# A scaled residual formed by two wide VectorE operations in place of four narrow ones

## The chip, the core and the metric

The kernel runs on one core of a Trainium2 chip. The metric is the device time of one execution in microseconds; the time given for a kernel is the median of its runs. Engines are named as the profile names them: PE is TensorE, DVE is VectorE, ACT is ScalarE, POOL is GpSimd.

## What is computed

A hybrid layer on 4 x 32 images of 128 x 128: Fourier layers with an attention over tokens, then a two-layer mixer, then attention and experts over rows. The part that the change touches is the first mixer layer:

```
def fno_layer(x, spec_w, skip_w, skip_b, out_shape, norm=None, act=None):
    xs = fourier_resample(conv1x1(x, skip_w, skip_b), out_shape)
    xf = spectral_conv(x, spec_w, out_shape)
    if norm is not None:
        xf = instance_norm(xf, *norm)
    y = xf + xs
    return act(y) if act is not None else y
...
m = fno_layer(m, mixer_w1, mixer_skip_w1, mixer_skip_b1, (H, W), norm=(mixer_norm_g1, mixer_norm_b1), act=_gelu)
```

With one channel, `conv1x1` is a scale and a shift of each image. The norms ahead of it are folded into the same two numbers, so `xs` is image times factor plus shift, with a factor and a shift per image. The inverse transform `xf` is added, and gelu follows.

## The kernel before

The kernel is a chain of stages, each a block with one program per engine; a stage starts when all engines have left the one before. The stage here is `stage_inverse` of kind 'mix1', between `stage_factors` and `stage_mixer`. The 128 images lie in SBUF as `m.b`, with 128 partitions (rows) and 128 columns an image. They are treated in 33 sets of images three apart: set b of quad q and remainder j holds images 12q+j, 12q+j+3 and so on; 30 sets hold four images, two hold three, one holds two. Three sets share one quad of the half-way result (eleven quads).

The order on each engine is written out by hand; semaphores tie the engines together. For a set b:

- DVE `linear(b)` (L1297) writes factor times image plus shift to `m.tmp`, which has two buffers, so it waits for the gelu of set b-2. The factor and the shift are columns 4 and 5 of `m.aff`, one number per image and the same on each partition.
- PE inverts the set into a bank of PSUM (L1177 to L1179, `second`); DVE `combine(b)` (L1331) adds gain times that to `m.tmp`.
- ACT takes gelu into `m.ust` (L1264), forms another scaled version of the images in place (`affine`, L1238), and copies out a forward transform (L1229).
- DVE takes statistics of the gelu (L1313); PE transforms it forward (L1187).
- POOL adds x from `m.a` to the images behind `affine` (L1143), then copies the gelu to `m.a` (L1146), which frees the buffer of `m.ust` for set b+2.
- Once in three sets the next quad's half-way result is split in two fp16 parts: ACT L1221, which stands behind the third set's gelu, affine and copy, then DVE L1282, which PE's next inversions need.

DVE's order is: linear(0), and then for each b linear(b+1), combine(b), statistics(b-1), and behind each third set L1282.

The names in the rows: `modes` is `m.tmp`, `images_b` is `m.b`, `transposed` holds `m.aff` and the statistics, `ow_stats_and_image_stage` is `m.ust`, `half_inverse_low` and `half_inverse_high` are the two halves.

Of the kernel before, what the change touches and what calls it, by code (L numbers as in the profile page):

```python
# [27 lines left out]
ALU = mybir.AluOpType  # L28
# [4 lines left out]
NB, NT, NH, NW = 4, 32, 128, 128  # L33
# [124 lines left out]
def over(ap, axis, n):  # L158

    shape = list(ap.shape)  # L160
    return ap.unsqueeze(axis).to_broadcast(shape[:axis] + [n] + shape[axis:])


def semaphores(nc, held, stage, names):

    made = {n: nc.alloc_semaphore(f"{stage}_{n}") for n in names.split()}
    held.extend(made.values())
    return Names(made)
# [872 lines left out]
def stage_inverse(nc, held, m, kind, mix=None, ins=None):  # L1041


    s = semaphores(nc, held, "inverse_" + kind, "in0 in1 in2 in3 v sized rooted total scaled turned high low first bhigh "
                   "blow rows used lin ready saved forward copied weights cleared algebra affine added gstat partly")
# [5 lines left out]
    def images(store, b):  # L1051
        q, j, gs = sets[b]
        return store[:, 12 * q + j:12 * q + j + 3 * len(gs) - 2:3, :]

    def width(b):
        return len(sets[b][2])

    def spread(flat, n):
        return flat[:, 0:n * NW].rearrange("p (t w) -> p t w", t=n)

    def turned(r):
        n = len(COEF_BANKS[r])
        return m.ps[2 + r % 6][0:FM, 0:n * P].rearrange("p (t x) -> p t x", x=n)
# [47 lines left out]
    with nc.Block() as block:  # L1111
        @block.sync
        def _(sp):
            if kind == 'proj':
                mix_img = mix.rearrange("t h w -> h t w")
                for q in range(QUADS):
                    if q >= 4:
                        sp.wait_ge(s.used, 3 * (q - 3))
                    t = slice(12 * q, min(NI, 12 * q + 12))
                    sp.dma_start(m.b[:, t, :], mix_img[:, t, :]).then_inc(arrived[q % 4], 16)  # L1120
                    if q == 3:
                        sp.wait_ge(s.cleared, 1)
                        load_mixer(sp, m, ins, 1, s.weights)
            if kind == 'mix1':
                x_img = ins['x'].rearrange("b t h w -> h (b t) w")
                for q in range(QUADS):
                    t = slice(12 * q, min(NI, 12 * q + 12))
                    if q >= 4:
                        sp.wait_ge(arrived[q % 4], 16 * (q // 4))
                    sp.dma_start(m.a[:, t, :], x_img[:, t, :]).then_inc(arrived[q % 4], 16)  # L1130
                load_mixer(sp, m, ins, 2, s.weights)
                sp.wait_ge(s.weights, 32)
# [142 lines left out]
        @block.vector  # L1275
        def _(vec):
            c = Chain(vec, s.v)

            def half(q):
                vec.wait_ge(s.bhigh, q + 1)  # L1280
                whole = min(4, (NI - 12 * q) // 3) * NW
                e = vec.tensor_tensor(m.halfL[:, q % 2, 0:whole], m.ps[q % 2][0:3 * FM, 0:whole], m.halfH[:, q % 2, 0:whole],  # L1282
                                      ALU.subtract)
                if q == QUADS - 1:
                    tail = slice(whole, whole + NW)
                    e = vec.tensor_tensor(m.halfL[0:2 * FM, q % 2, tail], m.ps[q % 2][0:2 * FM, tail],
                                          m.halfH[0:2 * FM, q % 2, tail], ALU.subtract)
                e.then_inc(s.blow, 1)

            def linear(b):  # L1290

                if b >= 2:
                    vec.wait_ge(s.ready, b - 1)
                q, j, gs = sets[b]
                for i in range(len(gs)):
                    img = 12 * q + j + 3 * i
                    e = vec.tensor_scalar(m.tmp[:, b % 2, i * NW:i * NW + NW], m.b[:, img, :], m.aff[:, 4, img:img + 1],  # L1297
                                          m.aff[:, 5, img:img + 1], ALU.mult, ALU.add)
                e.then_inc(s.lin, 1)

            def statistics(b):
                vec.wait_ge(s.used, b + 1)
                q, j, gs = sets[b]
                for i in range(len(gs)):
                    img = 12 * q + j + 3 * i
                    vec.bn_stats((m.st if kind == 'mix2' else m.stat)[:, img, :], m.b[:, img, :])

            def gelu_statistics(b):
                vec.wait_ge(s.ready, b + 1)
                q, j, gs = sets[b]  # L1310
                for i in range(len(gs)):
                    img = 12 * q + j + 3 * i
                    e = vec.bn_stats(m.stat[:, img, :], m.ust[:, b % 2, i, :])  # L1313
                e.then_inc(s.gstat, 1)

            def combine(b):
                vec.wait_ge(s.rows, b + 1)
                n = width(b)
                y = spread(m.ps[2 + b % 4], n)
                if kind == 'proj':  # L1320
                    if sets[b][1] == 0:
                        q = sets[b][0]
                        vec.wait_ge(arrived[q % 4], 16 * (q // 4 + 1))
                    x = images(m.b, b)
                elif kind == 'mix1':
                    vec.wait_ge(s.lin, b + 1)
                    x = spread(m.tmp[:, b % 2], n)
                else:
                    vec.wait_ge(s.partly, b + 1)
                    x = images(m.b, b)  # L1330
                vec.scalar_tensor_tensor(out=x, in0=y, scalar=gain, in1=x, op0=ALU.mult, op1=ALU.add).then_inc(s.used, 1)  # L1331

            if kind == 'proj':
                g = m.coef.rearrange("p x y -> p (x y)")
                vec.tensor_tensor_reduce(m.square, g, g, 1.0, 0.0, ALU.mult, ALU.add, m.col[:, 24:25]).then_inc(s.sized, 1)
                vec.wait_ge(s.total, 1)
                vec.tensor_scalar(m.col[:, 27:28], m.ps[0][:, 0:1], 2.0 ** -18, 1e-30, ALU.mult, ALU.add).then_inc(s.scaled, 1)
                vec.wait_ge(s.rooted, 1)
                vec.reciprocal(up, down).then_inc(s.scaled, 1)
                vec.wait_ge(s.scaled, 2)  # L1340
            for r, xs in enumerate(COEF_BANKS):
                vec.wait_ge(s.high, r + 1)
                n = len(xs)
                dst, high = (t[:, :, xs[0]:xs[0] + n] for t in (m.coefL, m.coefH))
                vec.scalar_tensor_tensor(out=dst, in0=turned(r), scalar=up[0:FM] if kind == 'proj' else 1.0, in1=high,
                                         op0=ALU.mult, op1=ALU.subtract).then_inc(s.low, 1)
            half(0)
            half(1)
            if kind == 'mix1':
                linear(0)  # L1350
            for b in range(len(sets)):
                if kind == 'mix1' and b + 1 < len(sets):
                    linear(b + 1)
                combine(b)
                if b >= 1:
                    (gelu_statistics if kind == 'mix1' else statistics)(b - 1)
                q, j, _ = sets[b]
                if j == 2 and q + 2 < QUADS:
                    half(q + 2)
            (gelu_statistics if kind == 'mix1' else statistics)(len(sets) - 1)  # L1360
# [1268 lines left out]
```

## Time and profile before

| what | value |
|---|---|
| median of three runs | 2350.61 us (2346.66 to 2353.24) |
| the profiled execution | 2354.32 us, span 2352.4 us |
| DVE busy in the span | 1882.0 us, 80% |
| PE busy | 2082.6 us, 89% |
| ACT busy | 1665.1 us, 71% |
| POOL busy | 602.9 us, 26% |

The stage of the change lasts from about 320 to 450 us of the span. The shares of the whole span say little on it, since most of the time belongs to the attention and the experts behind it; its own views are in the rows below. In a timeline, equal instructions of an engine that follow without a gap are merged: "x4" are four of them, and the time beside it runs from the start of the first to the end of the last. Two neighbours of an engine can overlap a little.

### The profile page before, as it was taken

The numbers are of one execution on the slowest core, as the hardware profiler recorded it, in microseconds if no ns is written. First come the engines' busy times: TensorE is split into PE (matmuls) and PEld (weight loads), VectorE is DVE, ScalarE is ACT, GpSimd is POOL, SyncE is SP. The second block draws the span as 40 slices with busy tenths as digits, with TensorE's granted clock in tenths as the row PEclk, the third lists the DMA queues.
The fourth block names the chain that finished last, engine by engine and source line by source line (L and its number), as shares of the span: only waits on it lengthen the run. The fifth ranks groups of instructions, "written<-read, shape, count | busy, mean of one in ns | idle before, by whom it ended". The sixth has DMA issues, their size and how long they took to land. (4 is left out here: it accounts for less than half of the span.)

```text
span 2352.4 us, 30833 instructions
## 1 busy us (share of the span) xinstructions
PE 2082.6 (89%) x10374; PEld 1067.8 (45%) x10374; DVE 1882.0 (80%) x3586; ACT 1665.1 (71%) x2413; POOL 602.9 (26%) x750
## 2 busy tenths in 40 slices
PE   7767859865899999999999999999999999767778
PEld 7722437732444444444444444444444444333333
DVE  4666887688778889889888888889888888867776
ACT  1444236464778888888888888878888888667666
POOL 1035415335302202102102102112000001046668
PEclk9978655555999999999999999999999999889999
DMA  9003560000000000000000000000000000000101
GB/s 301 9 1 143 153 151 3 1 1 6 1 10 1 1 1 1 1 1 1 1 1 1 1 1 1 1 1 1 1 1 1 1 1 1 0 14 28 32 28 46
DMA packets 80833, 55.72 MB, mean 24 GB/s; under 512 B 11283, under 2 KB 78739, under 8 KB 79140
## 3 DMA queue, kind: packets, MB, share of 16 engines
q1 hardware_dynamic: 75476, 52.38, 7.4%
q10 hardware_dynamic: 5200, 1.38, 0.3%
q8 instruction: 82, 1.34, 0.2%
q14 instruction: 75, 0.61, 0.1%
HBM read 36.91 MB, written 16.78 MB: 23 GB/s over the span
## 5 line engine op out<-in xcount | busy, mean ns | idle before, releaser
L2004 ACT ACTIVATE inner<-banks,key_bias,scales 128x1024 f32<-128x1024 f32 x512 | 617.2, 1205 | 212.5 <-PE banks L1821 207.3
L2189 DVE TENSOR_TENSOR weights_low<-weights,weights_high 128x1024 f16<-128x1024 f32 x512 | 674.4, 1317 | 17.0
L2011 ACT ACTIVATE weights<-inner 128x1024 f32<-128x1024 f32 x512 | 541.1, 1057 | 17.3 <-DVE weights_low L2189 1.6
L2185 DVE CAST weights_high<-weights 128x1024 f16<-128x1024 f32 x512 | 371.3, 725 | 175.8 <-ACT weights L2011 161.6
L2295 POOL CAST sums_high<-sums 128x512 f16<-128x512 f32 x32 | 39.1, 1221 | 1089.2 <-ACT sums L1983 1071.3
L1821 PE MATMUL banks<-queries_high,keys_high 128*128 128x512 f16 x1024 | 304.5, 379 | 0.7 <-ACT inner L2004 0.7
L1836 PE MATMUL banks<-weights_high,tokens_low 128*128 128x512 f16 x1024 | 304.6, 379 | 0.0
L1821 PE MATMUL banks<-queries_low,keys_high 128*128 128x512 f16 x1024 | 304.6, 379 | 0.0
L1821 PE MATMUL banks<-queries_high,keys_low 128*128 128x512 f16 x1024 | 304.6, 379 | 0.0
L1836 PE MATMUL banks<-weights_low,tokens_high 128*128 128x512 f16 x1024 | 304.6, 379 | 0.0
L1836 PE MATMUL banks<-weights_high,tokens_high 128*128 128x512 f16 x1024 | 304.5, 379 | 0.0
L2494 ACT ACTIVATE scaled<-banks,gates 128x128 f32<-128x128 f32 x512 | 149.2, 395 | 88.6 <-PE banks L2456 88.5
L1836 PEld LDWEIGHTS banks<-weights_high,tokens_low 128*128 128x128 f16 x1024 | 100.2, 98 | 120.9
L1821 PEld LDWEIGHTS banks<-queries_low,keys_high 128*128 128x128 f16 x1024 | 100.2, 98 | 120.9
L1836 PEld LDWEIGHTS banks<-weights_low,tokens_high 128*128 128x128 f16 x1024 | 100.2, 98 | 120.8
L1821 PEld LDWEIGHTS banks<-queries_high,keys_low 128*128 128x128 f16 x1024 | 100.2, 98 | 120.8
L1836 PEld LDWEIGHTS banks<-weights_high,tokens_high 128*128 128x128 f16 x1024 | 100.2, 98 | 120.8
L2454 PE MATMUL banks<-expert_weights_high,normed_high 128*128 128x512 f16 x256 | 103.3, 403 | 57.0 <-DVE residual_and_scaled L2530 43.7
L1821 PEld LDWEIGHTS banks<-queries_high,keys_high 128*128 128x128 f16 x1024 | 96.8, 98 | 91.3 <-ACT inner L2004 1.7
L2559 POOL TENSOR_TENSOR scaled_halves<-scaled 128x256 f32<-128x256 f32 x128 | 94.9, 741 | 93.4 <-ACT scaled L2494 93.0
L2530 DVE SCALAR_TENSOR_TENSOR residual_and_scaled<-banks,gates,residual_and_scaled 128x128 f32<-128x128 f32 x384 | 109.9, 341 | 0.1
L2455 PE MATMUL banks<-expert_weights_low,normed_high 128*128 128x512 f16 x256 | 103.2, 403 | 0.0
(613 smaller groups left out, 3243.0 us busy)
## 6 DMA issues: line engine op xcount, KB each, us to landing
images_b<-in_x SPq DMA_DIRECT2D x32, 256.0 KB, 9.4
images_a<-in_x SPq DMA_DIRECT2D x8, 1024.0 KB, 9.8
mixed_scratch<-images_a SPq DMA_DIRECT2D x4, 2048.0 KB, 13.1
result<-group_result SPq DMA_DIRECT2D x32, 256.0 KB, 2.3
images_b<-mixed_scratch SPq DMA_DIRECT2D x10, 768.0 KB, 5.2
images_a<-in_x SPq DMA_DIRECT2D x10, 768.0 KB, 9.1
mixer_weights<-in_L_conv_mixer_w SPq DMA_DIRECT2D x4, 272.0 KB, 6.8
table<-tables ACTq DMA_DIRECT2D x1, 772.5 KB, 7.1
```

Of the source, the lines that this page charges most:

```text
L1821: mm = pe.matmul(m.ps[2 * (t % 2) + h], key[:, par, part], query[:, q, 512 * h:512 * h + 512], start=(i == 0), stop=(i == 2))
L1836: mm = pe.matmul(m.ps[4 + h], value[:, par, k, :], weight[:, t % DEEP, 512 * h:512 * h + 512], start=(k == 0 and i == 0), stop=(k == KT - ...
L2004: act.activation(m.inner[:, t % 2, :], m.pair[t % 2], ACT.Exp, scale=m.fs[:, 1:2], bias=m.kb[:, c // QN % 2, k:k + 1]).then_inc(s.inner, 1)
L2011: act.activation(m.wt[:, t % 2, :], m.inner[:, t % 2, :], ACT.Exp).then_inc(s.outer, 1)
L2185: vec.tensor_copy(m.wH[:, t % DEEP, :], m.wt[:, t % 2, :]).then_inc(s.high, 1)
L2189: vec.tensor_tensor(m.wL[:, t % DEEP, :], m.wt[:, t % 2, :], m.wH[:, t % DEEP, :], ALU.subtract)\
L2295: after(pool.tensor_copy(m.oH[:, part], m.oS[:, part]))
L2454: pe.matmul(bank, m.lnH[:, t % RING, j, :], m.w8H[:, cols], start=True, stop=False)
L2455: pe.matmul(bank, m.lnH[:, t % RING, j, :], m.w8L[:, cols], start=False, stop=False)
L2494: o = act.activation(m.pb[:, n % 3, e, :], m.ps[ABANK[n % 2]][:, e * D:e * D + D], ACT.Copy, scale=m.gate[:, n, 4 + e:5 + e])
L2530: vec.scalar_tensor_tensor(out=m.u[:, n % 4, :], in0=m.ps[DBANK[n % 3]][:, e * D:e * D + D], scalar=m.gate[:, n, e:e + 1], in1=acc, op0=AL ...
L2559: pool.tensor_tensor(m.half[:, n % 2], m.pb[:, n % 3, 0:2], m.pb[:, n % 3, 2:4], ALU.add).then_inc(s.halved, 1)
```

## The change

`linear(b)` becomes two operations over all images of the set. The first multiplies the images with their factors, the second adds the shifts in place. The factor of an image is read as a second tensor operand: `over(...)` repeats it 128 times with a step of zero. `c.step` adds a wait of VectorE for its own product before the sum; the semaphore that tells `combine` is set by the sum.

```
-                for i in range(len(gs)):
-                    img = 12 * q + j + 3 * i
-                    e = vec.tensor_scalar(m.tmp[:, b % 2, i * NW:i * NW + NW], m.b[:, img, :], m.aff[:, 4, img:img + 1],
-                                          m.aff[:, 5, img:img + 1], ALU.mult, ALU.add)
-                e.then_inc(s.lin, 1)
+                n = len(gs)
+                scale, shift = (over(m.aff[:, k, 12 * q + j:12 * q + j + 3 * n - 2:3], 2, NW) for k in (4, 5))
+                x = spread(m.tmp[:, b % 2], n)
+                c.step(vec.tensor_tensor(x, images(m.b, b), scale, ALU.mult))
+                vec.tensor_tensor(x, x, shift, ALU.add).then_inc(s.lin, 1)
```

In the changed kernel the product has line 1298 and the sum line 1299; lines behind them keep their numbers. Every other engine's instructions are the same in the same order. On VectorE, in the middle of the stage from one L1282 over a quad, before:

```order
L1282 TENSOR_TENSOR half_inverse_low<-banks,half_inverse_high 102x512
L1297 TENSOR_SCALAR modes<-images_b,transposed 128x128 x4
L1331 SCALAR_TENSOR_TENSOR modes<-banks,small,modes 128x512
L1313 BN_STATS transposed<-row_stats_and_image_stage 128x6 x4
L1297 TENSOR_SCALAR modes<-images_b,transposed 128x128 x4
L1331 SCALAR_TENSOR_TENSOR modes<-banks,small,modes 128x512
```

and the same place on VectorE after the change:

```order
L1282 TENSOR_TENSOR half_inverse_low<-banks,half_inverse_high 102x512
L1298 TENSOR_TENSOR modes<-images_b,transposed 128x512
L1299 TENSOR_TENSOR modes<-modes,transposed 128x512
L1331 SCALAR_TENSOR_TENSOR modes<-banks,small,modes 128x512
L1313 BN_STATS transposed<-row_stats_and_image_stage 128x6 x4
L1298 TENSOR_TENSOR modes<-images_b,transposed 128x512
L1299 TENSOR_TENSOR modes<-modes,transposed 128x512
L1331 SCALAR_TENSOR_TENSOR modes<-banks,small,modes 128x512
```

Four instructions of 128 columns gave way to two of 512; nothing changed its place.

## Rows read from the trace of the kernel before

**Rows 1.** Busy time by stretch: us, busy us (instructions) of each engine, clock

```profile
350.00:400.00 50.00, 47.26 (x209) 35.32 (x209) 39.54 (x123) 33.57 (x87) 26.44 (x29) 0.50 0.09 17
```

**Rows 2.** Waits, 350 to 440 us: who for whom, total us, times, longest

```profile
ACT ow_stats_and_image_stage L1264 <- DVE modes L1331: 27.9, 16, 2.8
...
DVE half_inverse_low L1282 <- ACT half_inverse_high L1221: 14.7, 7, 2.1
```

**Rows 3.** Timelines of one period: start, length (us), instruction [idle before]

```profile
409.93 0.69 DVE L1282 TENSOR_TENSOR half_inverse_low<-banks,half_inverse_high 102x512 f16<-102x512 f32 x1 [2.09 <-ACT half_inverse_high L1221]
410.54 1.40 DVE L1297 TENSOR_SCALAR modes<-images_b,transposed 128x128 f32<-128x128 f32 x4
411.86 0.74 DVE L1331 SCALAR_TENSOR_TENSOR modes<-banks,small,modes 128x512 f32<-128x512 f32 x1
...
413.30 1.11 DVE L1297 TENSOR_SCALAR modes<-images_b,transposed 128x128 f32<-128x128 f32 x4
414.32 0.75 DVE L1331 SCALAR_TENSOR_TENSOR modes<-banks,small,modes 128x512 f32<-128x512 f32 x1
...
415.77 1.71 DVE L1297 TENSOR_SCALAR modes<-images_b,transposed 128x128 f32<-128x128 f32 x4
417.40 0.74 DVE L1331 SCALAR_TENSOR_TENSOR modes<-banks,small,modes 128x512 f32<-128x512 f32 x1
418.06 0.85 DVE L1313 BATCH_NORM_STATS2 transposed<-ow_stats_and_image_stage 128x6 f32<-128x128 f32 x4
421.02 0.69 DVE L1282 TENSOR_TENSOR half_inverse_low<-banks,half_inverse_high 102x512 f16<-102x512 f32 x1 [2.10 <-ACT half_inverse_high L1221]
...
418.17 0.63 ACT L1264 ACTIVATE ow_stats_and_image_stage<-modes 128x512 f32<-128x512 f32 x1 [0.75 <-DVE modes L1331]
418.71 1.64 ACT L1238 ACTIVATE images_b<-images_b,transposed 128x128 f32<-128x128 f32 x4
...
420.41 0.58 ACT L1221 CAST half_inverse_high<-banks 102x512 f16<-102x512 f32 x1
...
410.73 0.61 POOL L1146 COPY images_a<-ow_stats_and_image_stage 128x512 f32<-128x512 f32 x1
414.94 1.27 POOL L1143 TENSOR_TENSOR images_b<-images_b,images_a 128x512 f32<-128x512 f32 x1 [3.60 <-ACT images_b L1238]
416.28 0.61 POOL L1146 COPY images_a<-ow_stats_and_image_stage 128x512 f32<-128x512 f32 x1
```

**Rows 4.** Timeline: the first `linear`, the last L1282, the last GpSimd copy

```profile
332.22 2.13 DVE L1297 TENSOR_SCALAR modes<-images_b,transposed 128x128 f32<-128x128 f32 x8
...
432.05 0.42 DVE L1282 TENSOR_TENSOR half_inverse_low<-banks,half_inverse_high 102x256 f16<-102x256 f32 x1 [2.04 <-ACT half_inverse_high L1223]
...
449.12 0.40 POOL L1146 COPY images_a<-ow_stats_and_image_stage 128x256 f32<-128x256 f32 x1
```

**Rows 5.** The instructions of line 1297: ns min/median/max, first and last start

```profile
L1297 DVE TENSOR_SCALAR modes<-images_b,transposed x128: 332/341/751, 332.2 to 443.7; 128x128 f32<-128x128 f32 x128
```

**Rows 6.** Groups of VectorE, first 330 us: count | busy us, mean ns

```profile
L810 DVE TENSOR_TENSOR images_b<-transposed,pair 39x2048 f32<-39x2048 f32 x1 | 2.3, 2277 | 0.0
...
L819 DVE TENSOR_TENSOR images_b<-images_b 128x512 f32<-128x512 f32 x1 | 0.7, 693 | 0.0
```

**Rows 7.** Timelines of GpSimd and of VectorE in the attention stage, 573 us

```profile
572.99 1.03 POOL L2279 TENSOR_TENSOR centred<-images_b,token_factors 128x508 f32<-128x508 f32 x1 [19.70 <-POOLq L1615]
574.11 1.35 POOL L2281 TENSOR_TENSOR centred<-centred,token_factors 128x508 f32<-128x508 f32 x1
...
573.01 1.56 DVE L2163 TENSOR_TENSOR centred<-images_b,token_factors 128x508 f32<-128x508 f32 x1 [0.30 <-PEq L1615]
574.60 1.40 DVE L2164 TENSOR_TENSOR centred<-centred,token_factors 128x508 f32<-128x508 f32 x1
```

**Rows 8.** Timeline in the last stage, 2150 us

```profile
2150.22 0.43 DVE L2384 SCALAR_TENSOR_TENSOR gates<-ranks,exponentials 128x256 f32<-128x256 f32 x1
2150.36 0.87 POOL L2559 TENSOR_TENSOR scaled_halves<-scaled 128x256 f32<-128x256 f32 x1 [1.63 <-ACT scaled L2494]
```

## The prediction

> **What bounds the kernel now.** I read the views in this order: the busy time of the engines in the stage of the change, who waits there for whom, one period of the stage as a timeline, and then, all over the trace, wide VectorE operations that resemble the new ones.
>
> The change lives in one stage, the inverse transform of kind 'mix1', whose VectorE work starts at 332.22 us and whose last GpSimd copy starts at 449.12 us [rows 4], some 117 us of the span of 2352.4. TensorE is busy for 47.26 of 50 us there at a granted clock of 0.50, that is 1.2 GHz [rows 1], and looks like the bound. The waits say otherwise: between 350 and 440 us ScalarE stood 27.9 us before its gelu for VectorE's `combine` (L1331), and VectorE stood 14.7 us before L1282 for ScalarE [rows 2]. So these two hand the time to each other and TensorE runs ahead of them.
>
> The timeline shows the loop [rows 3]. The work repeats every three sets (a quad): L1282 starts at 409.93 and again at 421.02, a period of 11.09 us. In it VectorE does L1282, then three times linear (L1297), combine (L1331), statistics (L1313), with no gap between them. After the third combine (417.40, ends 418.14) ScalarE takes over: gelu 418.17, four affines 418.71 to 420.35, the fp16 half 420.41 to 420.99, and only then can VectorE do the next L1282. Every nanosecond that `linear` takes more or less therefore moves the period. Its work is not hidden anywhere; the idle 2.09 us before L1282 come behind it and shift with it.
>
> How long do four narrow operations take? I read it as the distance from the first L1297 to the combine behind it [rows 3]: set A (behind L1282) 410.54 to 411.86, 1.32 us; set B 413.30 to 414.32, 1.02 us; set C 415.77 to 417.40, 1.63 us. One narrow operation lasts 341 ns by the median, but up to 751 [rows 5], and in set B four of them fit in 1.11, so each starts some 257 ns behind the one before. A and C are longer because GpSimd is at work: its copy stands at 410.73 to 411.34 beside A, its sum 414.94 to 416.21 and its copy 416.28 to 416.89 beside C. Nothing of GpSimd's lies beside B. So two engines share something, and VectorE loses 0.3 us in A and 0.6 us in C.
>
> **The change, part by part.**
>
> Removed: 128 narrow operations in 33 sets (30 of four images, two of three, one of two). Added: 66 wide ones, two a set (L1298 the product, L1299 the sum), each over the whole set, with both operands in SBUF, and one wait between the two, since the sum reads what the product wrote. No other engine's row moves.
>
> *A wide operation by itself.* The nearest rows: L819, two SBUF operands, 128x512, its factor at a zero step, 693 ns; L810, 2048 columns with a zero step, 2277 ns [rows 6]. The slope is (2277 - 693) / 1536 = 1.03 ns a column, so 512 columns stream in 0.53 us behind 0.16 us of start. A zero step costs nothing in these rows. I take 0.69 us.
>
> *Spacing.* Neighbours without a wait overlap by 0.08 us (410.54 + 1.40 = 411.94 against 411.86) [rows 3]. With a wait between them there is a gap: L2163 ends at 574.57 and L2164 starts at 574.60 [rows 7]. So an undisturbed pair takes 0.69 + 0.03 + 0.61 = 1.33 us to the combine. In set B that is 1.33 - 1.02 = 0.31 us more.
>
> The Trainium skill ("VectorE: DVE Perf Modes", section on the DRAIN you can't avoid) says that a semaphore after each of a chain of operations costs nothing extra. These rows say 0.11 us for each. By the page the sum below would be some 1 us smaller (0.11 in each set B, and nothing in A and C, where the second operation stands for GpSimd anyway), 2356; the row decides.
>
> *Beside GpSimd.* Is a wide operation with two SBUF operands held up at all? L2163 and L2164 are (508 columns, expected 0.69) and took 1.56 and 1.40 us [rows 7]. GpSimd's L2279 ended at 574.02 and L2163 0.55 later, which is one streaming (0.53) behind GpSimd's end; L2281 ended at 575.46 and L2164 at 576.00, 0.54 behind. So a wide operation streams only once GpSimd's is over. It also works the other way round: L2281 started at 574.11 while L2163 streamed and took 1.35 us, where L2279 of the same form took 1.03. The extra 0.32 is the rest of L2163 (574.57 - 574.11 = 0.46) less 0.14, so GpSimd has 0.14 us of start before it wants to read. Who reads first goes first, and the other stands until it is done.
>
> Now the walk, in us from L1282's start.
> Set A: product 0.61 to 1.30, reading from 0.77. GpSimd's copy starts at 0.80, wants to read at 0.94, is held until 1.30, and ends 0.61 - 0.14 = 0.47 later, at 1.77. The sum starts at 1.33, is held until 1.77, ends at 2.30; combine starts at 2.22 instead of 1.93: 0.29 more.
> Set B: nothing of GpSimd's near (its next sum comes 0.13 behind the affines, which now end later too): 0.31 more.
> Set C, counted from its first operation: before, GpSimd's sum ended 0.44 us behind that point. It hangs on the affines of set A, which are 0.3 late, while C is 0.6 late, so it ends about 0.13 behind it. The product reads 0.16 to 0.69; the copy (from 0.20) is held, ends at 0.69 + 0.47 = 1.16; the sum streams 1.16 to 1.69; combine at 1.61 instead of 1.63: nothing gained or lost.
> One period: 0.29 + 0.31 - 0.02 = 0.58, call it 0.6 us more, 11.09 to about 11.67.
>
> *The whole stage.* At the start eight narrow ones take 2.13 us [rows 4] (2.05 to the combine); four wide ones 2.66: 0.6 more, and 0.3 more with the two sets up to the first L1282 of the loop, 0.9. The last L1282 stands at 432.05 [rows 4], two periods behind 409.93; eleven quads give nine of them inside the loop, so eight periods. 8 x 0.58 = 4.7. Behind it stand five sets of 4, 4, 3, 3 and 2 images; a wide pair over three takes 0.56 + 0.03 + 0.48 = 1.07 against 0.77; with GpSimd's copies giving back some of it, 0.8. Sum: 0.9 + 4.7 + 0.8 = 6.4 us. The stage's last GpSimd copy hangs on the last affine, and that on the last gelus, so all of it reaches the stage's end; behind it the next stage starts at once, nothing else being late.
>
> *Cover that stays.* GpSimd's copies are up to 0.4 us later each, but a gelu needs only the copy of two sets earlier. TensorE gets a period of 11.67 for the same work, so it is further from being the bound. No transfer is moved.
>
> Sum: the profiled execution took 2354.32 us (span 2352.4) and would take 2360.7. Against the median of the runs, 2350.61, it is **2357.0 us**, 0.27% more.
>
> **Bounds of the unknown.** The least known size is the sharing with GpSimd. If wide operations were never held, each set would cost 1.33: per period 4.0 against 3.97, near 0, with the start and end some 0.5 us in all. If they lose every race, see rival 1.
>
> **Rivals.**
>
> 1. *GpSimd's copy reads first: slower.* In A and C the product wants to read 0.03 us before the copy starts. If GpSimd takes hold with its start and not 0.14 later, and wins, then in A the product streams from 1.41 (the copy's end) to 1.94, the sum ends at 2.66, combine starts at 2.58: 0.65 more, not 0.29; C likewise 0.35 more, not 0. A period costs 1.3, the stage 6.4 + 10 x 0.7 = 13.4, so 2364 us. It decides at a shift of some 0.03 to 0.17 us. Against it: L2384 (256 columns, two SBUF operands, reading from 0.16 behind its start) was not held (0.43 us, 0.27 of streaming and 0.16) though GpSimd's L2559 had started 0.14 behind it [rows 8]. The Trainium skill ("SBUF — State Buffer", who interferes with whom) has the shared ports locked for the whole instruction by whoever issues first. By that rule L2163 would have kept L2281 out from its start, which fits, but the first product would also wait for GpSimd's sum (until 0.74), and the time would be as in this rival, near 2365. Chance 0.13.
>
> 2. *No sharing worth a mention: no change.* If a factor read again and again needs no second stream, the wide ones are never held; plus 0.5 to 1 us, 2351.5. Against it L2163, whose factor has a zero step too and was held. Chance 0.10.
>
> 3. *The zero step or the strided images read slowly.* Were each wide operation 0.3 us longer, 66 x 0.3 = 20 us, 2370. L819 and L810 speak against it. Chance 0.03.
>
> 4. *The later stages fall otherwise.* The granted clock of TensorE changes between its two levels later on, and the three runs of the kernel before lie 6.6 us apart with no change at all. A shift of a few us may meet a kinder moment: some 4 us less than the sum, 2353, and with the whole spread of those runs against me a little faster than before. Chance 0.09, of which 0.04 faster.
>
> The forecast itself, 5 to 8 us more, has 0.65.
>
> **How the numbers follow.** Something over 0.3%, 7.05 us, is about what a measurement of this kernel tells from no change, and my sum lies just below. Of the forecast's 0.65 I put 0.27 above 7.05 us and 0.38 below. Slower: 0.27 + 0.13 + 0.03 = 0.43. Faster: 0.04. Same: 0.38 + 0.10 + 0.05 = 0.53. The range runs from rival 2 to rival 1, 2351 to 2365; outside it stand rival 3, rival 4's faster side and the outer halves of rivals 1 and 2, together some 0.18.
>
> **What would show it.** In the profile after: L1298 and L1299 with an undisturbed 0.69 us each (0.66 to 0.72; 1.0 would be rival 3); the second of a pair beside the copy near 0.97 and the first never held (the first near 1.3 in A is rival 1, none held is rival 2); GpSimd's L1146 at 0.97 us in two sets of three; L1282 every 11.67 us, with the idle before it still 2.1; the gap between the pair 0.03. If the period is right and the total is not, the difference lies outside the stage, and that is rival 4. The forecast is wrong if the period stays below 11.4 or goes above 12.0.

## The result

The changed kernel took 2359.38 us (median of five runs, 2356.14 to 2361.26) against 2350.61 for the kernel before, 8.8 us more. The ratio is 1.0037, with a 95% interval from 1.0025 to 1.0049, so between 6 and 11.5 us slower. The profiled executions alone would mislead: their spans are 2354.2 and 2352.4 us. The stage of the change begins at 326.94 us in the one and at 332.22 in the other; the 5.3 us between them arose ahead of it, in code that is the same.

So the stage itself is what to look at. This is one period of the changed kernel, from one L1282 to the next, first the timeline of VectorE (start, length in us, instruction, count, and the idle time before it), then that of GpSimd. It answers to [rows 3].

```profile
409.15 0.69 DVE L1282 TENSOR_TENSOR half_inverse_low<-banks,half_inverse_high 102x512 f16<-102x512 f32 x1 [2.09 <-ACT half_inverse_high L1221]
409.75 0.68 DVE L1298 TENSOR_TENSOR modes<-images_b,transposed 128x512 f32<-128x512 f32 x1
410.47 0.98 DVE L1299 TENSOR_TENSOR modes<-modes,transposed 128x512 f32<-128x512 f32 x1
411.38 0.74 DVE L1331 SCALAR_TENSOR_TENSOR modes<-banks,small,modes 128x512 f32<-128x512 f32 x1
...
412.81 0.69 DVE L1298 TENSOR_TENSOR modes<-images_b,transposed 128x512 f32<-128x512 f32 x1
413.54 0.70 DVE L1299 TENSOR_TENSOR modes<-modes,transposed 128x512 f32<-128x512 f32 x1
414.15 0.75 DVE L1331 SCALAR_TENSOR_TENSOR modes<-banks,small,modes 128x512 f32<-128x512 f32 x1
...
415.59 0.69 DVE L1298 TENSOR_TENSOR modes<-images_b,transposed 128x512 f32<-128x512 f32 x1
416.31 0.98 DVE L1299 TENSOR_TENSOR modes<-modes,transposed 128x512 f32<-128x512 f32 x1
417.22 0.74 DVE L1331 SCALAR_TENSOR_TENSOR modes<-banks,small,modes 128x512 f32<-128x512 f32 x1
...
420.83 0.69 DVE L1282 TENSOR_TENSOR half_inverse_low<-banks,half_inverse_high 102x512 f16<-102x512 f32 x1 [2.09 <-ACT half_inverse_high L1221]
```

```profile
409.95 0.96 POOL L1146 COPY images_a<-ow_stats_and_image_stage 128x512 f32<-128x512 f32 x1
414.46 1.27 POOL L1143 TENSOR_TENSOR images_b<-images_b,images_a 128x512 f32<-128x512 f32 x1 [3.56 <-ACT images_b L1238]
415.79 0.95 POOL L1146 COPY images_a<-ow_stats_and_image_stage 128x512 f32<-128x512 f32 x1
```

The period is 420.83 - 409.15 = 11.68 us; it was 11.09. The idle time before L1282 is still 2.09 us, since it stands behind the linears. Read from the first operation of a linear to its combine: set A 411.38 - 409.75 = 1.63 (1.32 before), set B 414.15 - 412.81 = 1.34 (1.02), set C 417.22 - 415.59 = 1.63 (1.63). In A and C the sum L1299 takes 0.98 us and not the 0.69 of set B, and GpSimd's copy beside it 0.95 and not 0.61. The product is in none of the three sets longer than alone. So sets A and B each pay 0.3 us more than before; set C pays nothing, since the narrow form had lost 0.6 us there already.

That this is the rule and no accident of one period shows in the groups of the two lines (ns min/median/max, first and last start):

```profile
L1298 DVE TENSOR_TENSOR modes<-images_b,transposed x33: 529/686/797, 326.9 to 444.4; 128x512 f32<-128x512 f32 x30, 128x384 f32<-128x384 f32 x2, 128x256 f32<-128x256 f32 x1
...
L1299 DVE TENSOR_TENSOR modes<-modes,transposed x33: 691/978/981, 327.7 to 445.0; 128x512 f32<-128x512 f32 x30, 128x384 f32<-128x384 f32 x2, 128x256 f32<-128x256 f32 x1
...
L1146 POOL COPY images_a<-ow_stats_and_image_stage x33: 396/953/962, 334.0 to 450.4; 128x512 f32<-128x512 f32 x30, 128x384 f32<-128x384 f32 x2, 128x256 f32<-128x256 f32 x1
```

The median of the sums is the held length, that of the products the free one. TensorE has more idle time than before, 44.86 us busy of 50 where it had 47.26 [rows 1]:

```profile
350.00:400.00 50.00, 44.86 (x195) 33.67 (x196) 40.44 (x92) 30.54 (x79) 27.51 (x26) 0.50 0.00 1
```

From the first linear to the end of the last copy the stage took 450.79 - 326.94 = 123.9 us, against 449.52 - 332.22 = 117.3 before: 6.6 us more.

### The profile page after: what moved, and what is told of

Its sections match the earlier page's. It is cut to its first block and busy times, and to the rows that moved or that the text cites. A ratio compares the mean times of both kernels' runs of the same rounds, so it can differ in the third digit from the quotient of the medians.

```text
span 2354.2 us, 30771 instructions
## 1 busy us (share of the span) xinstructions
PE 2082.4 (88%) x10374; PEld 1069.0 (45%) x10374; DVE 1888.3 (80%) x3524; ACT 1665.0 (71%) x2413; POOL 609.7 (26%) x750
## 5 line engine op out<-in xcount | busy, mean ns | idle before, releaser
L2530 DVE SCALAR_TENSOR_TENSOR residual_and_scaled<-banks,gates,residual_and_scaled 128x128 f32<-128x128 f32 x384 | 110.1, 343 | 0.1
```

Of the source, the lines that this page charges most:

```text
L2530: vec.scalar_tensor_tensor(out=m.u[:, n % 4, :], in0=m.ps[DBANK[n % 3]][:, e * D:e * D + D], scalar=m.gate[:, n, e:e + 1], in1=acc, op0=AL ...
```

## The experiments

"Narrow" is the form of the kernel before (four operations a set), "wide" the changed one. "Stage" is the time from the first linear to the end of the stage's last instruction, a copy of ScalarE's (L1229); GpSimd's last copy, where it is left in, ends within 0.03 us of it. "Period" is the distance between two L1282 in the middle of the stage. Ratios are to the kernel before, run beside it. "Late" and "early" say where an instruction was moved; the sections tell.

| kernel | median us | kernel before beside it | ratio (95%) | period | stage |
|---|---|---|---|---|---|
| narrow (before) | 2350.61 | | | 11.09 | 117.3 |
| wide (the change) | 2359.38 | 2350.61 | 1.0037 (1.0025 to 1.0049) | 11.68 | 123.9 |
| wide, once more | 2359.13 | 2351.38 | 1.0035 (1.0023 to 1.0047) | 11.68 | 123.8 |
| narrow, linear late | 2346.67 | 2351.38 | 0.998 (0.997 to 0.999) | 10.53 | 112.8 |
| wide, linear late | 2349.05 | 2351.38 | 0.9989 (0.998 to 0.9998) | 10.83 | 116.4 |
| wide, product and sum apart | 2351.15 | 2351.38 | 1.0001 (0.9992 to 1.001) | 11.02 | 117.6 |
| narrow, no copy | 2344.44 | 2351.07 | 0.9973 (0.9962 to 0.9985) | 10.37 | 110.1 |
| wide, no copy | 2350.58 | 2351.07 | 0.9997 (0.9987 to 1.0006) | 11.10 | 118.1 |
| narrow, half early | 2341.57 | 2352.78 | 0.9958 (0.9946 to 0.9971) | 10.06 | 106.1 |
| wide, half early | 2343.43 | 2352.78 | 0.9967 (0.9954 to 0.998) | 10.07 | 109.3 |
| narrow, both moves | 2339.73 | 2352.78 | 0.9953 (0.9938 to 0.9968) | 10.28 and 9.75 in turn | 108.1 |

### The change once more

> The changed kernel once more, beside the kernel before. Theory 1 (all of the cost lies in the one stage, 0.6 us a period and 6.6 us in all, as the stage's first linear to its last copy lengthened from 117.3 to 123.9 us in the profiled executions): 6 to 8 us slower, ratio 1.0026 to 1.0034, the period between two L1282 again 11.68 us. Theory 2 (the first measured difference of 8.8 us holds 2 us that lie outside the stage): ratio 1.0037 or more, and stages behind it longer by 2 us against a profile of before.

Period 11.68 us eight times over, stage 123.8 us, 6.5 more than before: the profile repeats to a tenth of a microsecond. The time gave 1.0035, 7.8 us between the medians. The stage accounts for 6.5 of that; the time from the stage's end to the end of the span is 1901.3 us here, 1903.4 in the first profile of the change and 1902.9 before, so no profile shows 2 us more behind it. Single profiles differ by more than that in code that is the same: over the eleven profiles behind the table the first linear starts between 326.9 and 333.8 us, and the time behind the stage is 1898.9 to 1903.4 us. Theory 1 stands, and its 6.5 us lie inside both intervals, but the lower half of each. Whether a microsecond or two more is lost in executions that were not profiled stays open.

### Is it GpSimd's copy that holds the sum?

The copy is left out in both forms, so the images that a later stage reads are not the right ones.

```
-                    pool.tensor_tensor(images(m.b, b), images(m.b, b), images(m.a, b), ALU.add).then_inc(s.added, 1)
+                    pool.tensor_tensor(images(m.b, b), images(m.b, b), images(m.a, b), ALU.add).then_inc(s.saved, 1)
-                    pool.wait_ge(s.added, b + 1)
-                    pool.wait_ge(s.ready, b + 1)
-                    pool.tensor_copy(images(m.a, b), m.ust[:, b % 2, 0:width(b)]).then_inc(s.saved, 1)
```

> The kernel before without GpSimd's copy of the gelu (L1146), so the mixed images that a later stage reads are not the right ones; all else as before. If VectorE's extra 0.3 us beside the copy in set A and most of the 0.6 us in set C are holds by the copy, set A takes 1.02, set C about 1.2 (the sum of GpSimd stays), and the period falls from 11.09 to about 10.4 us: some 7 us faster. If the narrow operations are slow there for another reason, no change.

> The changed kernel without GpSimd's copy (the same part left out). Expected: all three linears 1.33 us, L1299 at 0.69 us everywhere, period 11.68 - 0.28 - 0.28 = 11.1 us, 0.5 to 1.5 us slower than the kernel before, and so some 7.5 us slower than the narrow form without the copy: more than the 6.6 us with the copy, since the narrow operations lose more by the copy than the wide ones. If the copy did not hold L1299, its 0.98 us would stay and the period would be 11.68.

VectorE's timeline over a period of the wide form without the copy (the lines are three lower, since three are gone ahead of them):

```profile
396.94 0.68 DVE L1295 TENSOR_TENSOR modes<-images_b,transposed 128x512 f32<-128x512 f32 x1
397.66 0.69 DVE L1296 TENSOR_TENSOR modes<-modes,transposed 128x512 f32<-128x512 f32 x1
398.27 0.74 DVE L1328 SCALAR_TENSOR_TENSOR modes<-banks,small,modes 128x512 f32<-128x512 f32 x1
...
402.48 0.69 DVE L1295 TENSOR_TENSOR modes<-images_b,transposed 128x512 f32<-128x512 f32 x1
403.21 0.69 DVE L1296 TENSOR_TENSOR modes<-modes,transposed 128x512 f32<-128x512 f32 x1
403.82 0.74 DVE L1328 SCALAR_TENSOR_TENSOR modes<-banks,small,modes 128x512 f32<-128x512 f32 x1
```

Every sum is at 0.69, every linear at 1.33 or 1.34, the period 11.10. And the narrow form:

```profile
395.11 1.10 DVE L1294 TENSOR_SCALAR modes<-images_b,transposed 128x128 f32<-128x128 f32 x4
396.13 0.74 DVE L1328 SCALAR_TENSOR_TENSOR modes<-banks,small,modes 128x512 f32<-128x512 f32 x1
...
400.04 1.30 DVE L1294 TENSOR_SCALAR modes<-images_b,transposed 128x128 f32<-128x128 f32 x4
401.26 0.74 DVE L1328 SCALAR_TENSOR_TENSOR modes<-banks,small,modes 128x512 f32<-128x512 f32 x1
```

Set A falls from 1.32 to 1.02 and set C from 1.63 to 1.22, where GpSimd's sum is left. So the copy held both forms, the narrow one more: without it the wide form is 8.0 us of stage behind the narrow one, with it 6.6. This rests on the profiles. The medians stand 6.1 us apart without the copy, where 7.5 had been expected, and 8.8 and 7.8 with it; their intervals are too wide to tell 6.6 from 8.0. The wide form had also been expected 0.5 to 1.5 us above the kernel before, and shows no difference from it.

The holds softened the change; they did not cause it. The cause is the price of a set that nothing holds, 1.34 us against 1.02: two passes over 512 columns at about 1.03 ns a column in place of one pass in four pieces that start 257 ns apart. With the copy in, sets A and B pay it, and in set C GpSimd had already taken more from the narrow form than the change costs.

### Does the place decide? VectorE's linear late

```
-                if kind == 'mix1' and b + 1 < len(sets):
-                    linear(b + 1)
                 combine(b)
+                if kind == 'mix1' and b + 1 < len(sets):
+                    linear(b + 1)
```

> The kernel before with one line moved: linear(b+1) is issued behind combine(b), not ahead of it. Nothing is left out. If linear stands on the loop that hands the time from VectorE to ScalarE and back, the one beside the third set falls into the 2.1 us that VectorE idles before L1282 and a period falls from 11.09 to 10.4 to 10.6 us, where TensorE becomes the next bound (47.26 us busy of 50 before): 4 to 7 us faster than before. If instead TensorE sets the pace already, no change.

> The changed kernel with the same line moved: linear(b+1) behind combine(b). Two of three linears a period still stand between two combines. Theory 1 expects a period of 10.7 to 10.9 us, so 0 to 3 us faster than the kernel before and 2 to 4 us slower than the narrow form with the move: the price of the wide form shrinks with what of it is hidden. A theory in which wide operations cost time wherever they stand (by slowing GpSimd or ScalarE) expects it to stay 6 to 9 us above the narrow form.

With linear(b+1) behind combine(b), the third linear of a period runs while ScalarE works toward the half. From the timeline of VectorE in the wide form:

```profile
400.96 0.73 DVE L1331 SCALAR_TENSOR_TENSOR modes<-banks,small,modes 128x512 f32<-128x512 f32 x1
401.61 1.07 DVE L1298 TENSOR_TENSOR modes<-images_b,transposed 128x512 f32<-128x512 f32 x1
402.71 0.69 DVE L1299 TENSOR_TENSOR modes<-modes,transposed 128x512 f32<-128x512 f32 x1
403.32 0.87 DVE L1313 BATCH_NORM_STATS2 transposed<-ow_stats_and_image_stage 128x6 f32<-128x128 f32 x4
404.56 0.69 DVE L1282 TENSOR_TENSOR half_inverse_low<-banks,half_inverse_high 102x512 f16<-102x512 f32 x1 [0.37 <-ACT half_inverse_high L1221]
```

Idle before L1282 is 0.37 us where it was 2.09. The periods are 10.83 and 10.53: the price of the wide form has shrunk from 0.6 to 0.3 us a period, 3.6 us of stage and 2.4 us between the medians. Both expectations held in period and time. In the first I took TensorE for the next bound; 10.53 us is still above what TensorE needs, as the half moved early shows below.

### The pair taken apart

```
-                c.step(vec.tensor_tensor(x, images(m.b, b), scale, ALU.mult))
+                vec.tensor_tensor(x, images(m.b, b), scale, ALU.mult).then_inc(s.v, 1)
+                if b >= 1:
+                    combine(b - 1)
+                vec.wait_ge(s.v, b + 1)
                 vec.tensor_tensor(x, x, shift, ALU.add).then_inc(s.lin, 1)
...
```

The loop, not shown, then calls `combine` itself only for the last set.

> The changed kernel with combine(b) issued between product and sum of set b+1, nothing left out. Product and sum are no neighbours, so the gap of 0.03 us turns to an overlap of 0.08, the copy of GpSimd can end beside combine (which reads one operand in SBUF, one in PSUM) and holds the sum for less, and the sum itself stands behind the combine. Expected period 10.9 to 11.1 us in place of 11.68, no difference from the kernel before (within 2 us). If the semaphore and the hold cost nothing, the period stays near 11.3: only the sum's place behind the third combine counts, 2 to 3 us slower than before.

```profile
396.07 0.68 DVE L1298 TENSOR_TENSOR modes<-images_b,transposed 128x512 f32<-128x512 f32 x1
396.67 0.74 DVE L1334 SCALAR_TENSOR_TENSOR modes<-banks,small,modes 128x512 f32<-128x512 f32 x1
397.33 0.68 DVE L1302 TENSOR_TENSOR modes<-modes,transposed 128x512 f32<-128x512 f32 x1
...
399.96 1.61 DVE L1302 TENSOR_TENSOR modes<-modes,transposed 128x512 f32<-128x512 f32 x1
```

The gap is gone: 396.07 + 0.68 = 396.75, and combine starts at 396.67. The period is 11.02 and the time that of the kernel before, as expected. One half of the reason was wrong. The sum is held for less only behind L1282, 0.68 us in place of 0.98; in the next set it now meets GpSimd's sum of images (on GpSimd's timeline 399.76 to 401.03) and takes 1.61 us, ending one streaming of 0.53 and a little behind the other's end, and in the third it takes 1.09. In all the holds cost a period 0.7 us more than in the changed kernel, and the three gaps that are gone give back 0.3. What paid was that the sum moved behind the combine: the idle time before L1282 fell from 2.09 to 1.07 us.

### The other end of the loop: ScalarE's half early

```
+                    q, j, _ = sets[b]
+                    if j == 2 and q + 2 < QUADS:
+                        half(q + 2)
                     affine(b)
                     if b >= 2:
                         copied(b - 2)
                 q, j, _ = sets[b]
-                if j == 2 and q + 2 < QUADS:
+                if kind != 'mix1' and j == 2 and q + 2 < QUADS:
                     half(q + 2)
```

> The kernel before with ScalarE's fp16 half (L1221) issued right behind the third set's gelu, ahead of its affines and its copy. Nothing is left out. VectorE then waits some 1.2 us for it and not 2.9, which takes up to 1.7 us from a period of 11.09 until TensorE's own work, 10.3 to 10.4 us a period, becomes the bound: period 10.3 on the average, 7 to 9 us faster than the kernel before. If ScalarE's tail were not part of the loop, no change.

> The changed kernel with the same move of ScalarE's half. Theory 1 (the wide form costs only where VectorE's chain sets the period): 11.68 less 1.7 would be 10.0, below TensorE's 10.3, so the period is 10.1 to 10.3 us, 6 to 8 us faster than the kernel before and only 0.5 to 2 us slower than the narrow form with the move, where the same two forms stand 6.5 us apart without it. A theory in which the wide form costs its 6.5 us wherever it stands expects 5 to 7 us between them.

> Both moves in the narrow form: linear(b+1) behind combine(b), and ScalarE's half ahead of the affines. If TensorE's 10.3 us a period is the bound once the half is early, the second move adds nothing: within 1.5 us of the narrow form with the early half alone. If it is not, the period falls below 10.2 all through.

Busy time from 350 to 400 us of the narrow and of the wide form with the half early (columns as in [rows 1]), each followed by a wait row of the same kernel (350 to 430 us):

```profile
350.00:400.00 50.00, 50.00 (x225) 39.41 (x225) 44.46 (x144) 38.57 (x98) 28.34 (x32) 0.50 0.12 24
...
ACT half_inverse_high L1221 <- PE banks L1166: 4.9, 7, 0.8
```

```profile
350.00:400.00 50.00, 50.00 (x225) 38.48 (x225) 47.52 (x110) 36.91 (x95) 29.02 (x30) 0.50 0.03 4
...
DVE half_inverse_low L1285 <- ACT half_inverse_high L1221: 2.7, 7, 0.4
```

TensorE is busy for all of the 50 us in both, and the two periods are 10.06 and 10.07 us: where the change cost 0.6 us a period, it now costs 0.01. The busy time alone would not show the bound, since TensorE had 49.48 of the 50 us in the narrow form with the late linear too, at a period of 10.53. In the narrow form with the half early, ScalarE waits for TensorE before each half, which it did not do there. In the wide one no such wait appears and VectorE still waits 0.4 us for the half, so there the chain of VectorE and ScalarE sets the period, and it happens to be about as long as TensorE's work.

The price has not gone; it is covered. The first two periods of the narrow form take 9.1 and 9.8 us, before TensorE holds it, while the wide form takes 10.07 from the first on: where TensorE still ran ahead, the wide form cost 1.0 us a period. The 3.2 us of stage that remain between the two lie in these first periods and at the ends. Between the medians are 1.9 us, as expected; against the kernel before the wide form is 9.3 us faster, where 6 to 8 had been expected.

This kernel, narrow with the half early, beats both: 2341.57 us, 11.2 us below the kernel before, where 7 to 9 had been expected. TensorE's need is about 10.0 us a period and not the 10.3 to 10.4 that I had put down. Both moves together gave the lowest median, 2339.73, 1.8 us lower where at most 1.5 had been expected, but with an interval that covers nearly the whole of the other's, a period of 10.01 us on average, and a profile in which the stage is 2 us longer (108.1 against 106.1) with VectorE busy all the time. I take the second move for unproven.

## Why the prediction came out as it did

The mechanism was right and the sum close. The range held the result. The likeliest case was "within 0.3%", the measured time is 0.37% up, in the case that had 0.43. The forecast's own band, 5 to 8 us more, holds the stage's 6.6 us and the second measurement, 7.8, but not the first, 8.8.

- *The bound.* VectorE and ScalarE hand the time to each other and TensorE runs ahead: shown by the late linear and the early half, which shorten the period without taking away any work.
- *Price of a wide operation*, 0.69 us with nothing for the zero step: 0.686 median, so rival 3 is out.
- *Spacing*, 1.33 for a free pair: 1.34 (set B). The gap between product and sum is 413.54 - 413.50 = 0.04 us where 0.03 was said, and neighbours without a wait overlap by 0.08. So here a wait for the operation just ahead cost about 0.11 us. The rule on the DRAIN from the Trainium skill ("VectorE: DVE Perf Modes") says that a semaphore behind each operation costs nothing; that fits the setting of one (the sum sets one, and combine starts 0.07 us before its end), not the wait.
- *The holds.* Forecast for the sum 0.97 and for the copy 0.97, in two sets of three: 0.98 and 0.95. Set A 1.63 for 1.61, set C 1.63 for 1.61. Rival 2 (no hold) is excluded by these rows, and so is the outcome of rival 1 (the product behind the copy). Whether GpSimd takes hold with its start or 0.14 us later stays open for a copy: in A the product begins to read at 409.75 + 0.16 = 409.91, and the copy starts at 409.95, too late to win in either case. The walk had that lead at 0.03 us, so a small shift would have tested it. The product was held only behind the loop (its longest, 797 ns, is the one behind the last L1282).
- *The sum.* Start to first L1282 of the loop: +0.9 for 0.9. Eight periods: (432.46 - 339.06) - (432.05 - 343.43) = 4.8 for 4.7. Tail: 18.33 - 17.47 = 0.9 for 0.8. Stage 6.6 for 6.4.
- *The step that was off* is the last one, from the stage to the measured time. I took the stage's 6.4 us as the whole and set it against a line of 7.05 us; two measurements gave 8.8 and 7.8. Their intervals include 6.6, and no profile shows time lost behind the stage, where the granted clock is the same before and after (0.88 from 450 to 1000 us, 0.98 behind that). Where the other 1 to 2 us lie stays open. With a forecast that close to the line, "same" and "slower" deserved equal chances.

## What to carry to other kernels

Fewer and wider operations are not cheaper by themselves: compare the distance from start to start, not the length. Four fused operations of 128 columns start 257 ns apart, 1.02 us for a set; two wide passes that each read a second operand cost 1.34. Before an edit on an engine that is not the busiest, find out whether the step stands on the loop that hands the time between engines; the same edit cost 0.6 us a period there and nothing a period once TensorE's work was as long. And look where the loop's idle time lies (here 2.1 us before L1282) and what ends it: issuing ScalarE's half ahead of its four affines and its copy was worth 11.2 us, more than the two forms of the arithmetic differ by.

## What the runs showed of the hardware that was not expected

The hold between VectorE and GpSimd goes by when an operation streams and not by when it starts. In the changed kernel the copy starts at 409.95 while the product (409.75 to 410.43) streams and takes 0.35 us longer than alone; the sum, started at 410.47, then ends 0.54 us behind the copy's end (410.91). In set C the product starts at 415.59, while GpSimd's sum of images, which started first, runs to 415.73; the product still takes 0.69 us, no more than alone. It begins to read some 0.16 us behind its start, at 415.75 (an estimate from the slope of [rows 6]), and nothing is left to wait for. Behind the last L1282 the product starts 0.24 us before the end of GpSimd's sum, and is held:

```profile
433.00 0.80 DVE L1298 TENSOR_TENSOR modes<-images_b,transposed 128x512 f32<-128x512 f32 x1
...
431.98 1.26 POOL L1143 TENSOR_TENSOR images_b<-images_b,images_a 128x512 f32<-128x512 f32 x1 [1.12 <-ACT images_b L1238]
```

The narrow operations are held too: a linear of four of them is seen at 1.11 us free and at 2.51 us in the narrow form with the late linear, where it meets both of GpSimd's operations:

```profile
398.13 1.11 DVE L1297 TENSOR_SCALAR modes<-images_b,transposed 128x128 f32<-128x128 f32 x4
...
400.58 2.51 DVE L1297 TENSOR_SCALAR modes<-images_b,transposed 128x128 f32<-128x128 f32 x4
```

But they hardly hold GpSimd in turn. Its copy took at most 0.63 us in the kernel before, where the median in the changed kernel is 0.95.
